# Latent attention: the next batch's norm turns and value products placed between the attention units, with a second value buffer, and the context keys beside the first products

## The reference, cut to what matters

```python
def _L1_xattn_ref(x, latents, mask, ln_x_g, ..., b_out):      # 4 heads of 64
    xn = layernorm(x, ln_x_g, ln_x_b)                        # context, 77 rows
    ln = layernorm(latents, ln_l_g, ln_l_b)                  # 1024 rows
    q = ln @ W_q
    kv = concatenate([xn @ W_kv, ln @ W_kv], axis=1)         # 1101 keys
    k, v = (kv[..., :INNER], kv[..., INNER:])
    qn = rmsnorm(q, q_gamma) * SCALE                         # per head
    kn = rmsnorm(k, k_gamma)
    sim = where(full_mask, einsum('bhid,bhjd->bhij', qn, kn), neg)
    out = einsum('bhij,bhjd->bhid', softmax(sim), v)
    return out @ W_out + b_out
x = x + _L1_xattn_ref(ctx_1024, _layernorm(x), mask, ...)
```

## Time and profile before

| what | us |
|---|---|
| median of 3 runs | 3894.58 (3892.18 to 3894.72) |
| the profiled execution, its own time | 3901.38 |
| its span, first to last instruction | 3899.6 |
| context part, first statistics to first norm turn | 2690.2 to 2721.4 |
| opening of batch 0, first norm turn to first scores | 2721.4 to 2768.1 |
| units of batches 0 to 3, first to last maximum | 97.7, 97.4, 98.4, 98.9 |
| between the units of two batches (last to first maximum) | 52.4, 55.4, 55.3 |

### The profile page before, as it was taken

The page is one execution under the profiler, slowest core; times in us unless marked ns, Lnnn a source line. Parts: engine busy times, 40 slices in busy tenths (PEclk is TensorE's granted clock), DMA queues, the critical chain, the costliest instruction groups (busy, mean ns, idle before and its releaser), DMA issues. The chain is left out here.

```text
span 3899.6 us, 58697 instructions
## 1 busy us (share of the span) xinstructions
PE 3319.5 (85%) x18960; PEld 2562.3 (66%) x18963; DVE 2929.8 (75%) x5839; ACT 2593.3 (67%) x3871; POOL 1806.3 (46%) x1098
## 2 busy tenths in 40 slices
PE   6877724169999999999999999995888888799999
PEld 4645521146777777777777777773666666699999
DVE  4567889779888888888888888994777676474347
ACT  2334545458888988898888989992667667354443
POOL 0034410016656566565665656650768576260015
PEclk9989956589999999999999999996999899799999
DMA  1046810038888888888888989892559468642224
GB/s 51 0 80 127 150 28 1 1 110 145 151 148 152 151 149 148 147 157 141 157 148 146 160 146 163 161 164 57 97 99 182 88 120 151 194 153 93 75 83 145
DMA packets 1571341, 469.87 MB, mean 120 GB/s; under 512 B 1507174, under 2 KB 1565159, under 8 KB 1569767
## 3 DMA queue, kind: packets, MB, share of 16 engines
q1 hardware_dynamic: 1564903, 449.40, 60.4%
q0 software_dynamic: 6144, 16.79, 1.3%
HBM read 49.00 MB, written 39.58 MB: 23 GB/s over the span
## 5 line engine op out<-in xcount | busy, mean ns | idle before, releaser
L2331 DVE TENSOR_REDUCE d_neg_max<-psum 128x1 f32<-128x1024 f32 x512 | 624.2, 1219 | 162.6 <-PE psum L2066 161.6
L2066 PE MATMUL psum<-d_KH,d_QH 128*128 128x512 f32 x2048 | 685.3, 416 | 25.4 <-DVE d_halves L2340 20.9
L2222 ACT ACTIVATE psum<-psum,d_bias 128x1024 f32<-128x1024 f32 x512 | 558.2, 1090 | 214.2 <-DVE d_bias L2335 204.4
L2340 DVE SCALAR_TENSOR_TENSOR d_halves<-psum,d_halves 128x1024 f16<-128x1024 f32 x512 | 624.2, 1219 | 31.9 <-ACT d_halves L2229 27.4
L2066 PE MATMUL psum<-d_KL,d_QH 128*128 128x512 f32 x2048 | 638.4, 393 | 0.0
L2066 PE MATMUL psum<-d_KH,d_QL 128*128 128x512 f32 x2048 | 637.0, 392 | 0.0
L2022 POOL TENSOR_TENSOR d_KC<-d_KC,d_tap_of 128x1024 f32<-128x1024 f32 x126 | 302.2, 2399 | 536.5 <-ACT d_tap_of L2211 536.5
L2229 ACT ACTIVATE d_halves<-psum 128x1024 f16<-128x1024 f32 x512 | 521.6, 1019 | 3.5
L2066 PEld LDWEIGHTS psum<-d_KH,d_QH 128*128 128x128 f32 x2048 | 357.0, 188 | 172.7 <-issue 68.5
L2066 PEld LDWEIGHTS psum<-d_KL,d_QH 128*128 128x128 f32 x2048 | 384.9, 188 | 87.8
L2066 PEld LDWEIGHTS psum<-d_KH,d_QL 128*128 128x128 f32 x2048 | 385.1, 188 | 87.3
(11 more groups left out here) (535 smaller groups left out, 7447.0 us busy)
## 6 DMA issues: line engine op xcount, KB each, us to landing
f_weights_raw<-in_L_ffn_packed_dram SPq DMA_DIRECT2D x10, 1088.0 KB, 16.0
f_tile<-expert_rows SPq DMA_DIRECT2D x71, 128.0 KB, 2.2
f_expert_out<-f_tile SPq DMA_DIRECT2D x71, 128.0 KB, 1.7
d_probsT<-d_halves SPq DMA_TRANSPOSE x512, 4.3
f_tile<-f_kept_rows SPq DMA_DIRECT2D x64, 128.0 KB, 2.1
expert_rows<-d_group_mixT SPq DMA_DIRECT2D x7, 1024.0 KB, 11.4
residual_stream<-in_x_dram SPq DMA_DIRECT2D x4, 1024.0 KB, 9.5
f_kept_rows<-residual_stream SPq DMA_DIRECT2D x4, 1024.0 KB, 8.5
```

What stands on the lines that cost most here:

```text
L2066: last = t.matmul(scores_at(u)[:, cols], q_part[:, ch, j * P:(j + 1) * P], k_part[hh % 2][:, ch, cols], start=k == 0, stop=k == 5)
L2222: a.activation(scores_at(u), scores_at(u), ACT.Exp, bias=bias[u % 2][:, 0:1], accum_out=sums[u // 4 % 4][:, u % 4, :]).then_inc(probs_read ...
L2331: v.tensor_reduce(neg_max[u % 2][:], scores_at(u), AXIS.X, ALU.max, negate=True)\
L2340: v.scalar_tensor_tensor(halves[u % 4][:, 1, :], scores_at(u), LIFT, halves[u % 4][:, 0, :], ALU.mult, ALU.subtract).then_inc(probs_low.se ...
```

## The change

In the second block, batches 1 to 3 no longer open with norm turns and no longer do values in their opening. PE's four groups of norm turns and ACT's moves of them stand at units 16, 18, 20 and 22 of the batch before, the eight value products, two at a time with one 512-wide high part on ACT and one on DVE, at units 24, 26, 28 and 30. Both go through bank 7, which the projections also use, so `project` waits for them and they wait for the sum of the projection before. Values alternate between two buffers. The applies move to units 12 to 19, statistics to 0 to 3, aggregates to 1 to 4, the power steps to 3 to 9; `add_bias` stays at 22 to 29. `raw` and `square` get a place of their own. Batch 0 does its values one tile a step beside the query/key products, in banks 6 and 7. The context keys' chain leaves the first block: sizes at the start of the second block, unit keys after step 1, turns and both parts at steps 9 and 10. `STEPS` goes from 14 to 11.

```diff
-        V = sb("V", [P, TB, H, 2 * HD], F16)
+        V0 = sb("V0", [P, TB, H, 2 * HD], F16)
+        V = [V0, sb("V1", [P, TB, H, 2 * HD], F16)]
+        raw = [sb(f"raw{i}", [P, G8, HD]) for i in range(3)]
+        square = sb("square", [P, G8, HD])
...
-        STEPS = TB + 6
+        STEPS = TB + 3
+        NORM_AT = {16 + 2 * k: k for k in range(4)}
+        VALUE_AT = {24 + 2 * k: k for k in range(4)}
...
+                def fill_free(b, u):
+                    if u >= 8:
+                        t.wait_ge(added.sem, added.at(2 * (PAIRS * b + (u - 8) // 2 + 1)))
                 def turn_norm(b, k):
-                    t.wait_ge(probs_ready.sem, probs_ready.at(U * b - (1 if k < 3 else 0)))
...
+                def turn_ctx(b):
+                    t.wait_ge(ctx_vec.sem, ctx_vec.at(5 * B + 5))
...
                 def multiply_qk(b, j):
+                    elif b:
+                        t.wait_ge(probs_ready.sem, probs_ready.at(U * b - 1))
...
                 def multiply_v(b, j):
-                    if j < 2:
-                        t.wait_ge(raw_ready.sem, raw_ready.at(TB * b + TB))
-                    else:
-                        t.wait_ge(v_low.sem, v_low.at(TB * b + j - 1))
+                    t.wait_ge(n.xT_ready.sem, n.xT_ready.at(4 * b + 4))
+                    if b == 0 and j >= 2:
+                        t.wait_ge(v_low.sem, v_low.at(j - 1))
...
                 def project(b, p):
+                    if b + 1 < B and 2 * p + 6 in NORM_AT:
+                        t.wait_ge(n.xT_ready.sem, n.xT_ready.at(4 * (b + 1) + NORM_AT[2 * p + 6] + 1))
+                    if b + 1 < B and 2 * p + 6 in VALUE_AT:
+                        t.wait_ge(v_low.sem, v_low.at(TB * (b + 1) + 2 * VALUE_AT[2 * p + 6] + 2))
...
                     for u in range(U):
                         scores(b, u)
                         behind(b, u)
+                        if b + 1 < B and u in NORM_AT:
+                            fill_free(b, u)
+                            turn_norm(b + 1, NORM_AT[u])
+                        if b + 1 < B and u in VALUE_AT:
+                            fill_free(b, u)
+                            multiply_v(b + 1, 2 * VALUE_AT[u])
+                            multiply_v(b + 1, 2 * VALUE_AT[u] + 1)
...
-                        if b + 1 < B and 9 <= u < 16:
-                            rstd_step(b + 1, u - 9)
+                        if b + 1 < B and 3 <= u < 10:
+                            rstd_step(b + 1, u - 3)
...
                 def move_raw(b, j):
-                    a.wait_ge(probs_low.sem, probs_low.at(U * b))
...
+                def value_pair_high(b, k):
+                    a.wait_ge(v_summed.sem, v_summed.at(TB * b + 2 * k + 2))
+                    a.activation(V[b % 2][:, 2 * k:2 * k + 2, :, 0:HD].rearrange("p t h e -> p (t h) e"),
+                                 bank(7).rearrange("p (m e) -> p m e", e=HD), ACT.Copy, scale=v_scale[:, 0:1])\
+                        .then_inc(v_high.sem, 2)
...
                     for u in range(U):
                         behind(b, u)
+                        if b + 1 < B and u in NORM_AT:
+                            move_norm(b + 1, NORM_AT[u])
+                        if b + 1 < B and u in VALUE_AT:
+                            value_pair_high(b + 1, VALUE_AT[u])
                         exps(U * b + u)
...
+                ctx_sizes()
...
+                        if b == 0 and 0 < s <= TB:
+                            value_low(s - 1)
...
+                        if b == 0 and s in (9, 10):
+                            ctx_key_low(2 * s - 18)
+                            ctx_key_low(2 * s - 17)
...
+                        if b == 0 and s == 1:
+                            ctx_units()
                     for u in range(U):
                         maximum(b, u)
+                        if b + 1 < B and u in VALUE_AT:
+                            value_pair_low(b + 1, VALUE_AT[u])
                         behind(b, u)
...
-                        if b + 1 < B and 22 <= u < 22 + TB:
-                            apply(b + 1, u - 22)
+                        if b + 1 < B and 12 <= u < 12 + TB:
+                            apply(b + 1, u - 12)
```

More of the change, by code:

```diff
@@ L2735, in _ @@
                                                 start=ch == 0, stop=ch == DC - 1)
-                        last.then_inc(ctx_pe.sem, 1)
-                    t.wait_ge(ctx_vec.sem, ctx_vec.at(5 * B + 5))
-                    for b in range(B):
-                        for h in range(H):
-                            twice = ctx_unit[:, b * H + h, :, :].rearrange("z a e -> z (a e)")
-                            last = t.transpose(PS[:, b * BANK + h * Z:b * BANK + (h + 1) * Z], twice,
-                                               core.ident[0:Z, 0:Z])
                         last.then_inc(ctx_pe.sem, 1)
@@ L2764, in _ @@
                                      ACT.Copy, scale=v_scale[0:Z, 0:1]).then_inc(ctx_act.sem, 1)
-                    for b in range(B):
-                        a.wait_ge(ctx_pe.sem, ctx_pe.at(DC + B + b + 1))
-                        a.activation(ctx_KH[:, b, :, 0:Z],
-                                     PS[:, b * BANK:b * BANK + H * Z].rearrange("p (h z) -> p h z", h=H), ACT.Copy,
-                                     scale=k_gamma[:, 0:1]).then_inc(ctx_act.sem, 1)
         loaded.passed(16 * LATER_LOADS)
@@ L2839, in turn_norm @@
                     t.wait_ge(n.normed.sem, n.normed.at(TB * b + 4 * half + 4))
-                    t.wait_ge(probs_ready.sem, probs_ready.at(U * b - (1 if k < 3 else 0)))
                     for q in range(4):
-                        last = t.transpose(bank(k)[:, q * P:(q + 1) * P], n.xn[:, 4 * half + q, ch * P:(ch + 1) * P],
-                                           core.ident[:])
+                        last = t.transpose(norm_bank(b, k)[:, q * P:(q + 1) * P],
+                                           n.xn[:, 4 * half + q, ch * P:(ch + 1) * P], core.ident[:])
                     last.then_inc(n.turned.sem, 1)
+                def turn_ctx(b):
+                    t.wait_ge(ctx_vec.sem, ctx_vec.at(5 * B + 5))
+                    t.wait_ge(raw_ready.sem, raw_ready.at(TB))
+                    t.wait_ge(v_low.sem, v_low.at(TB))
+                    for h in range(H):
+                        twice = ctx_unit[:, b * H + h, :, :].rearrange("z a e -> z (a e)")
+                        last = t.transpose(ctx_turned(b)[:, h * Z:(h + 1) * Z], twice, core.ident[0:Z, 0:Z])
+                    last.then_inc(ctx_pe.sem, 1)
                 def multiply_qk(b, j):
@@ L2904, in mix_values @@
                         for part in range(2):
-                            t.matmul(mix_bank, V[:, k, h, :], moving(part, k), start=k + part == 0, stop=False)
+                            t.matmul(mix_bank, V[b % 2][:, k, h, :], moving(part, k), start=k + part == 0, stop=False)
                     for part in range(2):
```

153 lines of the change are left out of this document (89 added, 64 removed).

## The result

The changed kernel takes 3875.28 us (median of 9 runs, 3871.37 to 3881.97), the kernel before, run beside it, 3893.36 (9 runs, 3888.10 to 3911.22). The ratio is 0.9948 with a 95% interval of 0.9934 to 0.9962: **20 us faster, 0.5%** (18 us by the two medians). The forecast was 16.6 us, at 3878.0. The profiled execution took 3875.28 (span 3873.5).

A forecast was written before the change was run, and what follows sets the result against it. Units were taken to wait mostly on DMA transposes, openings on a chain of small steps. Terms -11.2 + 2.2 - 9.0 - 12.0 - 11.9 + 17.3 + 8.0 = -16.6 us gave 3878.0 from the median 3894.58; range 3864 to 3892.

The forecast's parts named there:

- Openings 1 to 3: Openings of batches 1 to 3 without norm turns, values and the wait for moves: -9.0, -12.0 and -11.9 us.
- rivals B and D: B: openings 1 to 3 gated by last transposes, 3892 us, chance 0.14. D: units' pace absorbs every earlier start, 0.02.
- 43 to 44 us: Sign expected between one batch's last maximum and the next one's first, in place of 52 to 55 us.
- The clock: End of each opening: last turn and first scores at 1.2 GHz, +2.0 us in each of four, +8 in all.
- The first opening: Batch 0: context keys leave the first block, -11.2 us; values and keys beside the products, +2.2; clock, +2.0.
- steps 1 to 8 grow to 4.07: First opening: a value remainder adds 0.43 us to each VectorE step of 3.63.
- The keys' own cost in the opening: First opening: unit keys on the path, +2.3 us, and half of the remainders at steps 9 and 10, +1.1.
- The units: Fills between units of batches 0 to 2 (norm turns, applies, values): +5.75 us a batch, +17.3 in all.
- The step behind +2.2: Units with applies: VectorE's work brings four pairs from 6.2 to 6.8 us, +0.55 each, +2.2 a batch.
- Rival A: Fills between units hide and the clock holds: -35.9 us, or about -25 with one of the two; chance 0.25.
- rival C: Serial ring through bank 7 leaves all eight fills bare: 20.6 us a batch, slower at 3922 us; chance 0.09.
- the 98.9 of batch 3: Batch 3's units, with no next batch's work between them, were no faster, so units wait mostly on DMA transposes.

The follow-up runs named there:

- unread products: Changed kernel plus one product nobody reads behind TensorE's turns at steps 8, 9 and 10 of the openings of batches 1 to 3: 3874.45 us, ratio 0.9947.
- values at the end of the openings: Changed kernel with the value products of batches 1 to 3 back in their openings at steps 8 to 11, norm turns still between units: 3870.72 us, ratio 0.9952.

## Why the prediction was right, and where its terms were off

The time came 2.7 us from the forecast, within its range and with the sign. Most terms held. Two errors of 5 to 6 us went against each other, so that the total came this close is luck; that the change gains, and by which stretches, is not.

**Openings 1 to 3: right.** Forecast -9.0, -12.0, -11.9 with +2.0 of clock each; measured -6.9, -9.9, -9.8. All three are 45.5, so product, mixes and turns start as counted, and rivals B and D have nothing left: mix 14 began 4.2 after the last maximum, and mixes 14 and 15 didn't hold a thing. The mark "43 to 44 us" that I set for them had left the clock out, which the sum had; with the unread products they are 43.7 to 44.0. The difference of 3 us between batch 1 and the two others was no property of the place: in a second profile of the kernel before the first gap is 55.6 too (shown further below), so what the change gains there is 7 against the one execution and 10 against the other.

**The clock: about right.** The last two turns lost 0.9 each, and the scores of units 0 and 1 ran at 1.2 GHz (4.1 to 4.5 together, in place of 2.5), while those of unit 2 were at full clock again. By the experiment 1.5 to 1.8 us an opening can be had back, against 2.0 forecast. The Trainium skill, "TensorE: Matmul & The Clock Gate", section "HAM oscillation — how this bites in real kernels", which spoke against this change, says that waits between bursts lower the clock and each burst starts slow. The traces agree: behind the wait of 2.32 the turn fell to 1.2 GHz and the next two took 1.97, and the openings with unread products show how to keep out of it.

**The first opening: cheaper than forecast, and luck beside it.** Forecast -11.2 + 2.2 + 2.0 = -7.0; measured -12.7 - 1.0 + 0.4 = -13.3. From the first statistics to the first maximum after took 67.6 in this profile, 69.2 to 69.7 in the ten kernels of the experiments in which this part is the same; before took 80.9 and 78.4. By these means the gain is nearer to **10**: about 3 of the 6 us that the forecast missed are the clock of two single executions. After is the only one of the eleven in which norm turns and first product were both at full clock; in the others the turns took 2.4 to 3.6 in place of 1.94, and in four of them the product 3.78 in place of 1.98. In the profile of "values at the end of the openings" the same first product reads:

```profile
2710.54 3.78 PE L2844 MATMUL psum<-e_wqk,e_ln_xT 128*128 128x512 f32 x4 [1.07 <-ACT e_ln_xT L3032]
```

A part of the rest is the term "steps 1 to 8 grow to 4.07", which was too high. VectorE's timeline of after, from unit vectors to unit vectors, in the place of the earlier trace rows:

```profile
2726.23 1.21 DVE L3127 TENSOR_TENSOR e_unit<-e_raw,e_inv 128x1024 f32<-128x1024 f32 x1
2727.36 0.48 DVE L3148 SCALAR_TENSOR_TENSOR e_V<-psum,e_v_scale,e_V 128x256 f16<-128x256 f32 x1
...
2730.00 1.21 DVE L3127 TENSOR_TENSOR e_unit<-e_raw,e_inv 128x1024 f32<-128x1024 f32 x1
```

The step is 3.77: the value remainder adds its 0.43 as counted, but the unit vectors take 1.21 in place of 1.54, since they now fall behind POOL's bias addition (it ends at 2726.31, 0.08 after their start) and no longer beside it (2741.86, 0.46 after it). Four of the five steps are so and the first is 4.22: together 19.3 in place of 20.35, 1.0 us. The keys' own cost in the opening, 3.0 for 3.4, is another 0.4; what is left of the rest was not traced.

**The units: too cheap.** Forecast +5.75 a batch, measured +7.7, +7.75, +6.9. By its parts, for batch 0: applies in units 12 to 20 28.17 against 25.45, **+2.7** (forecast +2.2); units 24 to 30 23.47 against 20.35, **+3.1** (forecast +2.3; a pair takes 7.82, not 7.55); the last pair 3.36 against 1.76, **+1.6** (forecast 1.4); units 20 to 24, with two groups of norm turns more and two applies fewer, **+0.15** (forecast 0.2 - 0.35), and 0.85 to 1.0 less in the other batches. The step behind +2.2 is a sum that was added up wrongly: 3.5, 1.1, 1.8 and 0.7 for VectorE's work in a pair make 7.1, not 6.8, and the four pairs measured 7.04 each. Rival A (the fills hide) fell with this, rival C (they lie bare, 20.6 a batch) too. The applies of all three batches reach from 0.48 to 2.06 us with a mean of 1.25, which is also the mean of the 0.7 and 1.8 by turns that I had counted. An apply beside a low part was held up for the low part's rest: 4.95 for two applies beside 4.71 of POOL is the plainest row. The Trainium skill, "SBUF — State Buffer", section "SBUF: two separate sides", gives this as its rule, whole instructions excluding each other, and the row agrees. The same section names a second case, VectorE's modes that use both ports; the form with two scalars, held up to 1.89, would fit it, but no row here shows which mode it ran in. The premise that work between the units is mostly free was weaker than it looked, too: the 98.9 of batch 3, on which I built it, was the longest of fourteen profiles, whose mean is 96.2.

**What no step of the forecast holds.** Batch 3, whose units the change doesn't touch, took 4.0 less, and the end of the stage 1.4. Batch 3's units took 94.9 to 98.9 over all profiles, in the kernel before 98.9 and 96.4, so part of the 4.0, if not all, is scatter of one execution. Without both the table gives -17.4 against a forecast of -16.6: first opening 6.3 better, the three others 0.4 worse, units 5.1 worse. The end of the stage took 18.0 in both profiles of the kernel before, 15.5 to 17.0 in eleven of twelve with the change, and 18.5 in one; in before the last projections wait 4.18 us for ACT's move, in after 1.80. Why was not tested.

Still open besides: whether applies on ACT bring anything where nothing else is at its limit, and why batch 3's pace scatters by 4 us with equal code.

## What to carry to other kernels

Work that is moved out of a chain of small steps into a stretch that "waits for DMA" is free only until the next ring there closes: count the period of that ring (here products, high part, remainder, projection: 7.8 us) against the stretch's own pace (6.2 to 6.8), and look first whether the chain itself has waits on the engine that the work needs. Here the values fitted into TensorE's waits at the end of each opening, cost 1 to 2 us there in place of 4 to 8 in the units, and kept the clock up for the turns beside them. A small VectorE operation of the two forms tried here, beside long POOL operations, is to be costed at the POOL operation's rest, not at its own length, and two of them in a row at two whole POOL operations.

## What the runs showed of the hardware that was not expected

- The kernel before waits about 3 us for the moves before the first product of batch 1. In its first profile the wait was 2.97 and the product ran at full clock. I had expected a second profile of the same kernel to repeat the three gaps within 0.3; there the wait was 3.00 and the product took 3.78, at 1.2 GHz:

```profile
2872.89 3.78 PE L2851 MATMUL psum<-e_wqk,e_ln_xT 128*128 128x512 f32 x4 [3.00 <-ACT e_ln_xT L3014]
```

  The gap was 52.4 in the one and 55.6 in the other. I had laid 52.4 against 55.4 to the place, while it was the execution. Without that wait, after and the five kernels that left the openings alone have 45.5 in every one of their gaps.
- The clock's level at the start of the stage goes the same way: behind 3.19 us of idle the norm turns of after took 1.94, behind 2.87 those of the kernel with unread products 3.45. The shorter wait had the slower turns, so the length of the last wait alone does not set it. The first product of the kernel before says the same: behind 0.87 of idle it took 3.78 in one execution and 1.98 in the other.
- A VectorE operation holds up POOL too. POOL's floor took 0.28 in the first step of after and 1.11 to 1.16 in the later ones; while the unit keys' multiplication ran it took 3.31:

```profile
2716.52 2.46 DVE L3168 TENSOR_TENSOR e_ctx_unit<-e_ctx_raw,e_ctx_inv 77x2048 f32<-77x2048 f32 x1
2716.93 3.31 POOL L2957 TENSOR_SCALAR e_floor<-e_size 128x8 f32<-128x8 f32 x1
```

  It works on 128x8 elements: the size of an operation says little of how long it can be kept.
